# A gated cross-attention block: another order on a DMA queue, later first projections, and fillers and directly spread gates at the end

## The reference

```
xn   = layernorm(x)
q, k, v = xn @ wq.T + bq, ctx @ wk.T + bk, ctx @ wv.T + bv      # 16 heads of 8 features
attn = softmax(q k^T / sqrt(8)) v                               # 256 x 1601 per head
x    = x + tanh(g_xattn) * (attn @ wd.T + bd)
xf   = layernorm(x)
s    = sigmoid(xf @ gate_W) * route_scale                       # 8 experts, the best 2 kept,
gate = s[top 2] / sum(s[top 2])                                 # 0 elsewhere
x    = x + tanh(g_ffn) * (sum_e gate_e * (gelu(xf W1_e + b1_e) W2_e + b2_e)
                          + gelu(xf Ws1 + bs1) Ws2 + bs2)
```

## Time and profile before

| | before |
|---|---|
| median of 3 runs | 1282.12 us (1279.38 to 1286.63) |
| the profiled execution | 1285.7 us |
| its span, first to last instruction | 1283.6 us |
| TensorE matmuls busy | 1203.1 us, 94% |
| VectorE busy | 1060.8 us, 83% |
| ScalarE busy | 1050.8 us, 82% |
| GpSimd busy | 350.8 us, 27% |
| mean granted TensorE clock | 0.953 of full speed |

### The profile page before, as it was taken

One profiled execution on the slowest core, in us unless ns is written; L12 is line 12 of the kernel. 1 busy time (PEld: TensorE's weight loads), 2 busy tenths in 40 slices (PEclk: granted clock), 3 DMA queues, 4 the chain that ended last, 5 costly groups with the idle time before them and its releaser, 6 DMA issues.

```text
span 1283.6 us, 30942 instructions
## 1 busy us (share of the span) xinstructions
PE 1203.1 (94%) x12011; PEld 460.7 (36%) x12011; DVE 1060.8 (83%) x1346; ACT 1050.8 (82%) x1964; POOL 350.8 (27%) x359
## 2 busy tenths in 40 slices
PE   3698999999999999999999999999999999999877
PEld 1223333323334333343334333343334433343234
DVE  5888888879898998989898998889898899989112
ACT  1168879879998999889998899889998899889861
POOL 3461131504242043404233043413324032000100
PEclk7679989989999999999999999999999999999896
DMA  6983526454372545555462655545264655400100
GB/s 168 209 161 86 120 55 143 95 108 113 99 143 71 124 105 122 123 108 121 96 136 66 132 111 108 137 95 120 67 148 86 134 121 105 89 13 26 34 9 9
DMA packets 65587, 132.14 MB, mean 103 GB/s; under 512 B 13721, under 2 KB 40674, under 8 KB 62466
## 3 DMA queue, kind: packets, MB, share of 16 engines
q1 hardware_dynamic: 64510, 129.42, 45.8%
q10 hardware_dynamic: 932, 0.75, 0.2%
HBM read 86.59 MB, written 42.84 MB: 101 GB/s over the span
## 4 chain that ended last, share of the span: by engine, by line
PE 73%; DVE 9%; issue 6%; DMA 5%; ACT 3%; SPq 1%; POOL 1%; ACTq 0%; POOLq 0%; DVEq 0%
PE o_ps L1026 28%; PE a_ps L1008 16%; PE b_ps L990 13%; DVE run_max L1192 6%; PE a_ps L893 5%; PE a_ps L889 3%; DMA vctx<-ctx_t 3%; ACT probs L758 2%; PE a_ps L882 2%; PE b_ps L967 2%; PE b_ps L916 1%; PE a_ps L861 1%; DMA r_dram<-den 1%; ACT L773 1%; PE a_ps L873 1%
## 5 line engine op out<-in xcount | busy, mean ns | idle before, releaser
L758 ACT ACTIVATE probs<-a_ps 128x512 f32<-128x512 f32 (+1 forms) x1664 | 901.9, 595 | 121.2 <-PE a_ps L1008 106.9
L1192 DVE TENSOR_REDUCE run_max<-b_ps 128x2 f32<-128x1024 f32 x767 | 898.1, 1219 | 111.1 <-PE b_ps L990 103.2
L1026 PE MATMUL o_ps<-probs,v_op 128*32 128x256 f32 (+1 forms) x5368 | 507.5, 449 | 1.3 <-ACT probs L758 0.6
L1008 PE MATMUL a_ps<-q_op,k_op 51*128 51x256 bf16 (+1 forms) x3328 | 330.6, 277 | 18.5 <-ACT probs L758 14.6
L990 PE MATMUL b_ps<-k_op,q_op 48*128 48x512 bf16 x2046 | 316.0, 342 | 22.7 <-DVE run_max L1192 16.0
L1008 PEld LDWEIGHTS a_ps<-q_op,k_op 51*128 51x128 bf16 (+1 forms) x3328 | 108.2, 96 | 351.2 <-ACT probs L758 306.4
L1026 PEld LDWEIGHTS o_ps<-probs,v_op 128*32 128x32 f32 x5368 | 107.6, 108 | 188.0 <-issue 114.7
L990 PEld LDWEIGHTS b_ps<-k_op,q_op 48*128 48x128 bf16 x2046 | 87.2, 95 | 141.9 <-DVE run_max L1192 82.4
L653 POOL TENSOR_TENSOR k_parts<-k_t,one 128x400 bf16<-128x400 f32 (+1 forms) x60 | 51.4, 856 | 203.3 <-ACT k_t L779 202.1
L664 POOL TENSOR_TENSOR rstd_q<-rstd_q,minus_half 128x4 f32<-128x4 f32 x8 | 8.7, 1083 | 285.3 <-DVE rstd_q L1092 285.3
L893 PE MATMUL a_ps<-wv_s,vctx 128*128 128x128 f32 (+1 forms) x416 | 66.2, 301 | 5.9 <-DMA vctx<-ctx_t 4.5
(11 more groups left out here) (124 smaller groups left out, 597.8 us busy)
## 6 DMA issues: line engine op xcount, KB each, us to landing
k_op<-k_dram SPq DMA_DIRECT2D x62, 400.2 KB, 6.8
k_dram<-k_parts SPq DMA_DIRECT2D x30, 600.4 KB, 6.4
vctx<-ctx_t SPq DMA_DIRECT2D x16, 800.5 KB, 10.6
k_op<-k_dram SPq DMA_DIRECT2D x62, 200.1 KB, 7.5
kctx<-ctx_t SPq DMA_DIRECT2D x15, 800.5 KB, 4.9
o_dram<-o_s SPq DMA_DIRECT2D x30, 256.0 KB, 2.0
g_all<-g_dram SPq DMA_DIRECT2D x14, 512.0 KB, 6.4
k_dram<-k_parts SPq DMA_DIRECT2D x30, 200.1 KB, 5.8
```

Of the source, the lines that this page charges most:

```text
L758: act.activation(probs[0:keys, unit % PB, :], a_ps[at % AB][0:keys, :], ACT.Exp, scale=SCALE).then_inc(a_taken, 1)
L1008: last = pe.matmul(a_ps[(at + side) % AB][0:KEYS[t], SEQ * a:SEQ * a + SEQ], k_op[buf][rows, slot, 128 * t:128 * t + KEYS[t]], q_op[buf][r ...
L1026: last = pe.matmul(o_ps[32 * j:32 * j + 32, cols], v_op[s // 2 % 2][0:KEYS[t], t, GP * (s % 2) + j, :], probs[0:KEYS[t], unit % PB, cols], ...
L1192: dve.tensor_reduce(run_max[:, t, :, p, c:c + 1].rearrange("q v o -> q (v o)"), slot[:, :, :], AX.X, ALU.max).then_inc(b_taken, 1)
```

## The change

1. In even steps SP loads the values' context first, then spreads the sums, then loads the operands of step s+3.
2. The first values' context (batch 0) is loaded behind the store of the third key group (`store_group(2)`), where it stood ahead of it, and the four value projections of batch 0 stand ahead of the row scores 8, 11, 14 and 17 in the place of 3, 6, 9 and 12.
3. In step 31 two output tiles of the FFN instead of four, with Y and Z apart; the other two follow the last dense product.
4. `last_output` takes FG's place in the order and spreads the gates directly from `g_tok` (tokens on partitions): a column of gates, repeated 64 times, is the stationary operand of a product with the identity, eight such products for a group of two experts. FG's transposes move between the second and third group. They still serve the biases and the shared expert. `pick_s` and its load go.
5. Behind the last V, OT 1, AT, the last Z and FT, TensorE runs fillers (`keep_busy(n)`: n products of a bf16 identity with 256 columns into a part of `b_ps[0]` that nobody reads).

```diff
@@ -52,6 +52,8 @@
 FULL = GP * QTILES * RUNS
 SUNITS = FULL + QTILES
 S_AHEAD = 10
+
+BUSY = {"V": 6, "OT": 5, "AT": 4, "FY": 8, "FT": 5}
 S_TURN = 4
 
 
@@ -157,7 +159,7 @@
 
     events = [("S", n) for n in range(SUNITS)]
     for i in range(4):
-        events.insert(events.index(("S", 3 * i + 3)), ("A", ("V", 0, i)))
+        events.insert(events.index(("S", 3 * i + 8)), ("A", ("V", 0, i)))
         events.insert(events.index(("S", 2 * i + 13)), ("A", ("K", 1, i)))
     return events, [("A", ("T", 0, 0))] + [("S", n) for n in range(SUNITS, SUNITS + S_TURN)]
 
@@ -193,14 +195,16 @@
     c, b = CHUNKS - 1, BATCH - 1
     during = ORDER[STEPS - 1]
     during.insert(len(during) // 3, ("B", ("OT", 0, 0)))
-    for i in range(4):
-        at = len(during) * (9 + i) // 14
-        during[at:at] = [("Y", ("FY", c - 1, i)), ("Z", ("FY", c - 1, i))]
+    for i in range(2):
+        for at, half in enumerate("YZ"):
+            during.insert(len(during) * (16 + 6 * i + 3 * at) // 32, (half, ("FY", c - 1, i)))
     ORDER[STEPS] = [e for e in ORDER[STEPS] if e[0] in "VW"] + [("B", ("OT", 1, 0)), ("A", ("AT", b, 0)),
                                                                ("B", ("D", b, 0))]
+    ORDER[STEPS] += [(half, ("FY", c - 1, i)) for i in (2, 3) for half in "YZ"]
     ORDER[STEPS + 1] = [("A", ("FT", c, 0)), ("A", ("FL", c, 0))]
-    ORDER[STEPS + 2] = [("A", ("FH", c, i)) for i in range(GELU_TILES + 1)] + [("A", ("FG", c, 0))]
-    for s in range(STEPS + 3, LAST + 1):
+    ORDER[STEPS + 2] = [("A", ("FH", c, i)) for i in range(GELU_TILES + 1)]
+    ORDER[STEPS + 3] = [("A", ("FG", c, 0))]
+    for s in range(STEPS + 4, LAST + 1):
         ORDER[s] = []
 
 
@@ -346,7 +350,6 @@
         hid_s = sb("hid_s", [HID + EXPERTS + 1, CHUNK])
         g_t, spare = hid_s[HID:HID + EXPERTS, :], sb("spare", [1, 1])
         y_s = sb("y_s", [128, 4, 128])
-        pick_s = sb("pick_s", [HID + EXPERTS, GELU_TILES, 128])
         sum_inv, attn_tok = sb("sum_inv", [128, 4, 4]), sb("attn_tok", [128, QTILES, 2, 2, GP, DH])
 
         key_in, first_in, const_in, ones_set = (sem(n) for n in ("key_in", "first_in", "const_in", "ones_set"))
@@ -379,7 +382,7 @@
         folds = [(gx_s, g_attn), (gf_s, g_ffn), (bv_s, bv), (wd_s, wd), (bd_s, bd)]
         consts = [(route_s, route), (earlier, earlier_in),
                   (gate_s, gate_w), (w1_s, w1), (ws1_s, ws1), (w2_s, w2), (ws2_s[0:HID, :], ws2),
-                  (ws2_s[HID:HID + EXPERTS + 1, :], b2s), (pick_s[HID:HID + EXPERTS], pick_in), (b1_s, b1), (bs1_s, bs1)]
+                  (ws2_s[HID:HID + EXPERTS + 1, :], b2s), (b1_s, b1), (bs1_s, bs1)]
 
         def keys_split(engine, b):
 
@@ -591,8 +594,8 @@
             store_group(0)
             store_queries(sp, 0, [1], q0_written)
             load_group(0)
+            store_group(2)
             load(vctx, ctx_t[0]).then_inc(vctx_in, 16)
-            store_group(2)
             store_group(1)
             load_group(2)
             load_context("K", kctx, 1, kctx_in)
@@ -612,12 +615,12 @@
                     move_maxima(sp, 0, [0])
                 if s % 2 == 1 and 0 < b + 2 < BATCH:
                     store_keys(b + 2)
-                if 2 <= s + 3 < STEPS:
-                    load_operands(s + 3)
                 if s % 2 == 0 and 0 < b + 1 < BATCH:
                     load_context("V", vctx, b + 1, vctx_in)
                 if s % 2 == 0 and 0 <= b - 1 < BATCH - 1:
                     spread_sums(b - 1)
+                if 2 <= s + 3 < STEPS:
+                    load_operands(s + 3)
                 if s % 4 == 2 and 0 <= (s - 6) // 4 < CHUNKS - 1:
                     spread_gates((s - 6) // 4)
                 if 0 < s + 1 < STEPS:
@@ -926,36 +929,56 @@
                     last = pe.transpose(slot[:, 0, 128 * i:128 * i + 128], o_s[h][:, cols], ident[:, :])
                 last.then_inc(b_filled, 1)
 
+            def keep_busy(n):
+
+                for _ in range(n):
+                    pe.matmul(b_ps[0][:, 1, 256:512], ident_b[:, :],
+                              ident_b[:, :].unsqueeze(1).broadcast_to([128, 2, 128]), start=True, stop=True)
+
             def last_output():
 
 
+                c = CHUNKS - 1
+                at = A_AT["FG", c, 0]
+                banks = [o_ps, a_ps[(at + 1) % AB], a_ps[(at + 2) % AB], o_ps]
                 y = [b_ps[i // 2][:, i % 2, 0:128] for i in range(4)]
                 toks = [slice(128 * i, 128 * i + 128) for i in range(4)]
 
                 def spread(m):
-                    if m >= AB:
-                        pe.wait_ge(pick_taken, m + 1 - AB)
-                    pe.matmul(a_ps[m % AB][:, :], pick_s[HID:HID + EXPERTS, m, :], g_t, start=True,
-                              stop=True).then_inc(pick_filled, 1)
+                    if m in (1, 2):
+                        pe.wait_ge(a_taken, at + m + 1 - AB)
+                    if m == 3:
+                        pe.wait_ge(pick_taken, 1)
+                    for t in range(4):
+                        for e in range(2):
+                            gates = g_tok[:, t, 2 * m + e:2 * m + e + 1].broadcast_to([128, HID])
+                            last = pe.matmul(banks[m][HID * e:HID * e + HID, toks[t]], gates, ident[:, :],
+                                             start=True, stop=True)
+                    last.then_inc(pick_filled, 1)
 
                 def grow(m):
                     pe.wait_ge(pick_taken, m + 1)
                     for i in range(4):
-                        last = pe.matmul(y[i], hid[:, m, toks[i]], w2_s[:, m, :], start=False,
+                        last = pe.matmul(y[i], hid[:, m, toks[i]], w2_s[:, m, :], start=(m == 0),
                                          stop=(m == GELU_TILES - 1), skip_group_check=True)
                         if m == GELU_TILES - 1:
                             last.then_inc(y_filled, 1)
 
-                pe.wait_ge(a_taken, a_done("FG", CHUNKS - 1))
+                pe.wait_ge(gate_seq, GATE_OPS * CHUNKS)
+                pe.wait_ge(o_copied, STEPS)
                 spread(0)
+                spread(1)
                 pe.wait_ge(b_taken, max(B_DONE.values()))
+                grow(0)
+                spread(2)
+                grow(1)
+                a_unit("FG", c, 0)
+                spread(3)
+                grow(2)
+                pe.wait_ge(a_taken, a_done("FG", c))
                 for i in range(4):
-                    pe.matmul(y[i], hid_s[:, toks[i]], ws2_s[:, :], start=True, stop=False, skip_group_check=True)
-                spread(1)
-                for m in range(GELU_TILES):
-                    grow(m)
-                    if m + 2 < GELU_TILES:
-                        spread(m + 2)
+                    pe.matmul(y[i], hid_s[:, toks[i]], ws2_s[:, :], start=False, stop=False, skip_group_check=True)
+                grow(3)
 
             def ffn_output(c, i, half):
                 tok = slice(128 * i, 128 * i + 128)
@@ -1049,15 +1072,25 @@
                         values(unit, [0, 1])
                     elif kind == "S":
                         row_scores(unit)
+                    elif unit == ("FG", CHUNKS - 1, 0):
+                        last_output()
                     elif kind == "A":
                         a_unit(*unit)
+                        if s >= STEPS and unit[0] in BUSY:
+                            keep_busy(BUSY[unit[0]])
                     elif unit[0] == "OT":
+                        if unit[1] == 1:
+                            pe.wait_ge(b_taken, b_done("D", BATCH - 2))
+                            keep_busy(BUSY["V"])
                         turn_outputs(unit[1])
+                        if unit[1] == 1:
+                            keep_busy(BUSY["OT"])
                     elif kind == "B":
                         dense(unit[1])
                     else:
                         ffn_output(unit[1], unit[2], "YZ".index(kind))
-            last_output()
+                        if unit == ("FY", CHUNKS - 2, 3) and kind == "Z":
+                            keep_busy(BUSY["FY"])
 
 
         @block.vector
@@ -1115,9 +1148,12 @@
 
             def last_output():
 
+                at = A_AT["FG", CHUNKS - 1, 0]
+                banks = [o_ps, a_ps[(at + 1) % AB], a_ps[(at + 2) % AB], o_ps]
                 for m in range(GELU_TILES):
+                    dve.wait_ge(a_taken, a_done("FH", CHUNKS - 1, m))
                     dve.wait_ge(pick_filled, m + 1)
-                    dve.tensor_tensor(hid[:, m, :], hid[:, m, :], a_ps[m % AB][:, :], ALU.mult).then_inc(pick_taken, 1)
+                    dve.tensor_tensor(hid[:, m, :], hid[:, m, :], banks[m][:, :], ALU.mult).then_inc(pick_taken, 1)
                 dve.wait_ge(out_done, 16 * (CHUNKS - 1))
                 for i in range(4):
                     dve.wait_ge(y_filled, i + 1)
```

## The result

The changed kernel takes 1262.55 us (median of four, 1261.74 to 1265.94), the kernel before beside it 1282.07 us: ratio 0.9849, 95% interval 0.9815 to 0.9883, 19.5 us faster where 15.9 were forecast. The forecast of 1270 us started from the profiled execution, 3.6 us above the median; that is half of the 7.3 us by which it lies too high. The profiled execution takes 1265.9 us, its span is 1263.9 us, and its mean granted clock 0.975 instead of 0.953.

A forecast was written before the change was run, and what follows sets the result against it. TensorE was taken to bound the kernel (73% of the last-ending chain), only its stands and half clock being winnable. Terms 6.0 + 1.5 + 2.5 + 5.9 = 15.9 us off the profiled 1285.7 gave 1270 us, range 1262 to 1281.

The forecast's parts named there:

- the likeliest case: Whole kernel: the forecast itself, 1270 us, alone 1264 to 1275, chance 0.52.
- part 1: Even steps, SP's queue: earlier context removes 4.5 us of TensorE waits and 1.5 us of half-clock loss; 6.0 us.
- The rival that the context was hidden anyway: Middle: ScalarE or VectorE take the 4.5 us back, the even-step reorder gives 0; 1276 us, chance 0.09.
- The maxima do not come late: Six steps with gates: the last row of maxima still lands before the next score pair; counted as nothing.
- the margin of 1.6 us: Step 6: last row of maxima reckoned to land at 333.6, its score pair having run at 335.19.
- the sign that I had named as making the prediction wrong: Step 6: score pairs waiting for the six maxima issues, expected at about 328 in the old time.
- the third rival in its mild form: Six steps with gates: row of maxima lands 1 us late; 1276 us, chance 0.12.
- Part 2: Beginning: first queries load earlier, gaining 2.5 us, moved value projections cost 1.0; 1.5 us gained, bounds -4 and +4.
- Part 3: Last score step: two halved output tiles instead of four whole cut ScalarE's stands from 4.5 to 2.0 us; 2.5 gained.
- Part 4: End: fillers keep TensorE's clock full and the gates spread directly; 5.9 us gained.
- (c): End, after last gelu: a spread costs 2.1 us, stretch to last addition falls from 16.0 to 13.8; 2.2 us gained.
- The rival of the clock falling in the spreads: End: clock drops to half during gate spreading; 1276 us, or about 1289 with whole end at half clock; chance 0.22.

The follow-up runs named there:

- Part 1 alone: Kernel before with only SP's new even-step order (context, sums, operands): 1278.8 us, ratio 0.9987 to the kernel before.
- with part 2: Kernel before with the new even-step order and the later first values' context, last step and end unchanged: 1278.4 us, ratio 0.9990.
- the gate: Changed kernel, GpSimd splitting the fourth key quarter only after VectorE split the maxima (steps 4, 8, ..., 24): 1261.4 us, again 1258.8 us.
- the third group: Last set of runs on one chip: kernel before 1281.4 us, unaltered changed kernel 1262.0 us, and three variants beside them.

## Why the prediction was right

The time was in the range and the likeliest case came, but by luck in part: part 1 was counted at 6.0 us and gave next to nothing, and the end gave more than was counted for it. Two errors cancel.

- **Part 1, 6.0 us: wrong.** The step that failed is that the 4.5 us of context waits would be won. They went, but the same order brings the sums to GpSimd early, and its splitting meets VectorE's: 8.4 us more of waits for the maxima. Part 1 alone gives 0 to 4 us, and with part 2 nothing that can be measured. I had written of the new order only who would come late; nobody was asked who would come early. The rival that the context was hidden anyway has the right size with another mechanism. On top of all other parts the order is worth 5 to 8 us, by the split all of it half clock; why it is worth more there than alone stays open.
- **The maxima do not come late: nearly right, with the margin wrong.** The order of issues was right to 0.5 us, but the margin of 1.6 us is not there: the last row took at least 3.2 us to land where I had taken 2.0, the median of the outputs' store, and by the weight loads it comes within the last 0.84 us or too late. In the steps 22 and 26 TensorE stands 0.67 and 0.90 us for it, the sign that I had named as making the prediction wrong. It is the third rival in its mild form, in two of six steps and at 1.6 us in all; the second profile of the changed kernel has 0.19 us of it.
- **Part 2, +1.5 us: not confirmed.** The queries' wait fell by 3.5 us, more than the 2.5 I took; but I left out that the context, behind a store, lands at 36.65 only, that row scores queue behind the projection that waits for it, and that the third key group's load is behind it too. Step 0 ended 1.8 us later in this pair of profiles, and undoing the part changes nothing at step 31. The medians leave 0 to 2 us for it.
- **Part 3, 2.5 us: right.** The stands fell from 4.5 to 2.84 us, 1.7 instead of 2.5, and the last score step gained 2 to 3 us by the profiles of the kernels that differ in it. The 5.65 us of the two main profiles hold 3.6 us more, half clock from 1208 to 1221.5 that shrank to 3 us; it lies ahead of the tiles, so that is luck and not the change. What the sum left out is that the two moved tiles are worth some 3 us at the end as well, where I had only asked whether they fit.
- **Part 4, 5.9 us: right mechanism, too small.** The clock stayed at 1.00, the tiles and fillers fitted; the moved tiles did more of that than the fillers. The mis-sized term is (c): a spread takes 1.09 us where I costed 2.1, so four give 4 us; the end won 10.8 us, of it 6.7 in (c) where I had 2.2. The rival of the clock falling in the spreads did not come: the windows have 1.00. My 0.13 us an instruction came from products with 128 result columns; these have 64. Of the Trainium skill's 81 ns (TensorE: Matmul & The Clock Gate, section Back-to-back issue gap) I had said that the row did not bear it out; for these products the trace lies below it, at 65 ns.

The sum of what was shown: about 0 to 3 us in the middle, 12 (profiles) to 16 (medians) behind step 31.

## What to carry to other kernels

When a transfer is brought forward, ask what starts earlier through it and on whose cover it lands, not only what comes late. Split each time into span times clock and half clock before looking for stands, but check the price of a microsecond of half clock among executions of one kernel first. Here most of what paid did so by keeping TensorE fed in a thin stretch, and of the 7 to 8 us of stands that the gate took away 3 were left in the time. Before a difference between two profiles is put down to an edit, look whether it begins ahead of the edited instructions, and whether a second profile has it. The last few per cent of the span, where nothing else is in flight, were worth more than all the middle.

## What the runs showed of the hardware

- Two elementwise operations on VectorE with 16 elements a partition last 0.85 and 0.70 us beside GpSimd's of 0.85 to 0.94 us, 0.17 us without (steps 4, 8, ..., 24, with and without the gate).
- fp32 products of 128 moving columns into 64 result columns follow each other at 0.065 us when they alternate between the two halves, at 0.10 us when they do not; into 128 columns at 0.13 us (1.06 us for eight).
- A row of 2 KB issued behind 512 KB of gates landed at least 3.2 us after its issue; the median of the 256 KB stores of the outputs was 2.0 us.
- The clock falls in one execution and not in the next of the same kernel: in the third group the unaltered changed kernel has 50 to 58 us of half clock in six executions, the kernel before 82 to 110 in seventeen. Of it 47 to 59 us lie in the first 84 us of every profile. One wait of 0.96 us, in all fourteen profiles, is followed by some 10 us of half clock in two.
